# Second attention: two of the three row products of the RMS norm on GpSimd become one scaled copy with bias on ScalarE

## The chip, the cores and the metric

The kernel runs on one core of a Trainium2 chip. The metric is the device time of one execution in microseconds (us), lower is better. Engines are named as the profile has them: PE is TensorE (PEld its weight loads), DVE is VectorE, ACT is ScalarE, POOL is GpSimd, SP is SyncE, whose queue (SPq) issues every DMA of this kernel.

## What is computed

The reference is a stream of 32 batches of 112 rows by 256 features through four layers:

```
x = x + attention_1(layernorm(x), ctx)          # one head of 256
x = x + ffn_1(layernorm(x))                     # three blocks of two quantised layers with adapters
x = x + attention_2(ctx, layernorm(x))          # x gives the queries, ctx (375 rows) keys and values, 16 heads of 16
x = x + ffn_2(layernorm(x))                     # ternary weights, 256 -> 1024 -> 256
```

What the change touches is the entry of ffn_2. Its input is normalised twice, by the layer norm of the stream and by the RMS norm inside the first bitlinear:

```
x_hat = (x - mean) / sqrt(var + 1e-5)                    # layernorm
v     = mean(x_hat ** 2)
y     = x_hat * rsqrt(v + 1e-8) * norm1_w                # rmsnorm, then rounding to 8 bit levels
```

For one row both norms together are y = (x * rs - mean * rs) * norm1_w, with one scalar rs for each row that comes from mean and var alone.

## The kernel before

The kernel is written out by hand, engine by engine: each engine has its own program, and counting semaphores tie them. It has four stages with a barrier between them, except that stage 4 (ffn_2) follows on stage 3 (attention_2) without one. In the profiled execution stage 3 lies from about 700 to 1100 us, and stage 4 from there to the end.

Stage 3 is a loop over the 32 batches, `step3(b, ...)` on PE, ACT and DVE, `moves(b)` on SP and `rows3(b)` on GpSimd, with three buffers of keys and queries (`ks`, `qs`). In one step of batch b:

- PE makes the scores of batch b for 12 units u = 0 to 11 (4 heads by 125 context rows each; line 1751), and, between them, the scores of batches b + 1 and b + 2 from which the row maxima are taken (`scores_for_max`, line 1735); it weighs the values with the exponentials, two units at a time (`weigh`, line 1765; the last pair of a step is units 10 and 11), and finishes batch b - 1 (transposes, and the product with w_out, lines 1776, 1782, 1495).
- ACT makes the exponentials, one instruction for each unit (`exps`, line 954). Between them it copies the weighed values of b - 1 out (`pv_out`, line 958, ahead of u = 0), the turned heads (`o_out`, line 962, after u = 3) and the rows of negated maxima of b + 1 (`m_out`, line 966, after u = 8).
- DVE takes the 16 row maxima (line 1281), normalises the heads of b - 1, adds them to the stream (`x4`, line 1306), and takes the statistics of the new rows (`stats4`, `aggregate4`, `keep4`, lines 1311, 1316, 1320).
- SP, in this order: `rows_m(b + 1)` (waits for `m_out`), 12 loads of the keys and queries of b + 3 (`load_half`, lines 510 and 513), `store_y(b - 2)` (line 538), `store_x(b - 1)` (line 532).
- GpSimd: `norm_y` of a batch, `lay_v` (the values of a batch to come are laid out, line 728, and the output bias is added to its rows, line 732), `factors4` (eight small products that make rs and mean * rs of a batch, lines 746 to 753, each waiting for the one in front).

The row b of the stream `xs` is stored to DRAM as x (for the last residual), then normalised in place, and stored again as y (`normed_rows_dram`). `norm_y(b)` makes the three products in place, and its first one waits until the store of x has landed (semaphore `x_stored`). Stage 4 reads y and x back as tiles of 128 rows. The last steps of stage 3 hand over to stage 4: `store_y(28)` comes in SP's order ahead of the loads of the ffn_2 weights (`ternary_w_dram`), for which PE's first transpose of stage 4 (`in_turn(0)`, line 1828) waits. ACT's program at the hand-over is `pv_out(31)`, `xq_out(0)`, `o_out(31)`, `relu(0)`, `xq_out(1)`, `square(0)`, and then the tiles of stage 4 (`xq_out` line 980, `relu` 993, `square` 999, `squares` 1006, `hq_out` 1011). DVE's `activate` (line 1375) waits for `square`.

The helper `apart(eng, passed)` is a semaphore increment that no one waits for; it only sets two waits apart in the instruction stream. `over_thirds` runs step 0, a loop of nine turns of three steps, and the rest (steps 28 to 31) written out.

Of the kernel before, what the change touches and what calls it, by code (L numbers as in the profile page):

```python
# [8 lines left out]
ALU = mybir.AluOpType  # L9
ACT = mybir.ActivationFunctionType  # L10
AX_X = mybir.AxisListType.X
P = 128
# [5 lines left out]
def xattn_ffn_kernel(  # L18
# [5 lines left out]
    B, L, D = x.shape  # L24
# [33 lines left out]
    with ExitStack() as ctx:  # L58
        def alloc(stack, name, shape, dt=F32):
            return stack.enter_context(nc.sbuf_tensor(name, shape, dt))  # L60

        def sb(name, shape, dt=F32):
            return alloc(ctx, name, shape, dt)

        def sem(name):
            return ctx.enter_context(nc.semaphore(name))


        xs = sb("x_stream", [L, B, D])
# [12 lines left out]
        k4 = sb("ffn2_constants", [P, 2])  # L82
        eps4 = sb("eps4", [P, 2])
        ones3 = sb("ones3", [P, L], BF16)

# [101 lines left out]
        at = [0]  # L187
# [85 lines left out]
        def sems(names):  # L273
            return [sem(n) for n in names.split()]
# [12 lines left out]
        passed_pool, passed_dve, passed_sp = sems("passed_pool passed_dve passed_sp")  # L287
        ENG = ("pe", "act", "dve", "pool", "sp")
        stage_done = {e: sem(f"stage_done_{e}") for e in ENG}

        def stage_end(eng, me, n):
# [49 lines left out]
            "x_plus_bout_made pads_zeroed ffn2_row_factor_steps")  # L341

        (x_stored, y_stored, y_tiles_in, x_tiles_in, ternary_w_stored, ffn2_weights_in, ffn2_constants_made,
         y_made, x_factor_steps, x_rounded, x_int_turned, x_intT_ready, hidden_made, relu_made,
         squares_made, activation_made, hidden_weighted, square_sum_made, hidden_root_steps,
         hidden_factor_steps, hidden_factor_made, hidden_rounded, hidden_int_turned, hidden_intT_ready,
         ffn2_out_made, result_made) = sems(
            "x_stored y_stored y_tiles_in x_tiles_in ternary_w_stored ffn2_weights_in ffn2_constants_made "
            "y_made x_factor_steps x_rounded x_int_turned x_intT_ready hidden_made relu_made "
            "squares_made activation_made hidden_weighted square_sum_made hidden_root_steps "  # L350
            "hidden_factor_steps hidden_factor_made hidden_rounded hidden_int_turned hidden_intT_ready "
            "ffn2_out_made result_made")
# [265 lines left out]
        def _(pool):  # L618
# [114 lines left out]
            def factors4(b):  # L733


                chained = [0]

                def link(ins):
                    chained[0] += 1
                    ins.then_inc(ffn2_row_factor_steps, 1)  # L740
                    pool.wait_ge(ffn2_row_factor_steps, 10 * b + chained[0])
                    apart(pool, passed_pool)
                v, at = mv4[:, row(b), 1], row(b)
                pool.wait_ge(ffn2_row_stats, 3 * b + 3)
                apart(pool, passed_pool)
                link(pool.tensor_tensor(t4[:, at], v, eps4[0:L, 0:1], ALU.add))
                link(pool.tensor_tensor(rs4[:, at], t4[:, at], mhalf[0:L, 0:1], ALU.pow))
                link(pool.tensor_tensor(t4[:, at], v, rs4[:, at], ALU.mult))
                link(pool.tensor_tensor(t4[:, at], t4[:, at], rs4[:, at], ALU.mult))
                link(pool.tensor_tensor(t4[:, at], t4[:, at], eps4[0:L, 1:2], ALU.add))  # L750
                link(pool.tensor_tensor(rr4[:, at], t4[:, at], mhalf[0:L, 0:1], ALU.pow))
                link(pool.tensor_tensor(rs4[:, at], rs4[:, at], rr4[:, at], ALU.mult))
                link(pool.tensor_tensor(rr4[:, at], mv4[:, row(b), 0], rs4[:, at], ALU.mult))

            def norm_y(b):

                x_row = xs[:, row(b), :].rearrange("p o d -> p (o d)")
                pool.wait_ge(x_stored, 16 * (b + 1))
                apart(pool, passed_pool)
                pool.tensor_tensor(x_row, x_row, rs4[:, row(b)].broadcast_to([L, D]), ALU.mult).then_inc(ffn2_row_factor_steps, 1)  # L760
                pool.wait_ge(ffn2_row_factor_steps, 10 * b + 9)
                apart(pool, passed_pool)
                pool.tensor_tensor(x_row, x_row, rr4[:, row(b)].broadcast_to([L, D]), ALU.subtract).then_inc(ffn2_row_factor_steps, 1)
                pool.wait_ge(ffn2_row_factor_steps, 10 * b + 10)
                apart(pool, passed_pool)
                pool.tensor_tensor(x_row, x_row, n1_bc[0:L, :], ALU.mult).then_inc(y_made, 1)


            pool.tensor_tensor(k4[:, 0:1], wmean[:, 0:1], wmean[:, 0:1], ALU.mult).then_inc(ffn2_constants_made, 1)
            pool.tensor_scalar(k4[:, 1:2], wmean[:, 1:2], 1.0 / 127.0, None, ALU.mult).then_inc(ffn2_constants_made, 1)  # L770
            pool.wait_ge(ffn2_constants_made, 2)
# [64 lines left out]
        def _(act):  # L836
# [127 lines left out]
            def m_out(b):  # L964
                act.wait_ge(minus_max_turned, b + 1)
                act.activation(mrow[:, :], M3, ACT.Copy).then_inc(minus_max_rows_ready, 1)

            def step3(b, par, n):
                if not isinstance(b, int) or b >= 1:
                    pv_out(b - 1)  # L970
                for u in range(12):
                    exps(b, u)
                    if u == 3 and (not isinstance(b, int) or b >= 1):
                        o_out(b - 1)
                    if u == 8 and (not isinstance(b, int) or b < B - 1):
                        m_out(b + 1)
            def xq_out(i, par):

                act.wait_ge(x_int_turned, i + 1)
                act.activation(xqT, XT4[par], ACT.Copy, bias=-ROUND).then_inc(x_intT_ready, 1)  # L980

            m_out(0)
            over_thirds(act, step3)
            pv_out(B - 1)
            xq_out(0, 0)
            o_out(B - 1)


            def relu(i, par):
                if not isinstance(i, int) or i >= 2:  # L990
                    act.wait_ge(hidden_weighted, i - 1)
                act.wait_ge(hidden_made, i + 1)
                act.activation(th[par], H4[par], ACT.Relu, scale=am4[par][:, 8:9]).then_inc(relu_made, 1)  # L993
# [19 lines left out]
            def step4(i, par, n):  # L1013
# [18 lines left out]
        def _(dve):  # L1032
            chain = [0]

            def link(ins):
                chain[0] += 1
                ins.then_inc(dve_setup_steps, 1)
                dve.wait_ge(dve_setup_steps, chain[0])
# [283 lines left out]
            def step3(b, par, n):  # L1322

                later = not isinstance(b, int) or b >= 1
                last = (par + 2) % 3
                for k in range(H):
                    if k < H - AHEAD:
                        if not isinstance(b, int) or b < B - 1:
                            maxima(b + 1, k + AHEAD)
                    elif not isinstance(b, int) or b < B - 2:  # L1330
                        maxima(b + 2, k - (H - AHEAD))
                    if later and k == 1:
                        norm_o(b - 1)
# [103 lines left out]
                    inverse_x(i + 3, 1 - par)  # L1437

            over_thirds(dve, step3)
            dve.wait_ge(ffn2_constants_made, 3)  # L1440
            dve.wait_ge(y_tiles_in, 16)
            for i in range(2):
                max_x(i, i)
# [462 lines left out]
```

## Time and profile before

| what | value |
|---|---|
| time, median of 3 runs | 1274.8 us (1268.82 to 1278.72) |
| time of the profiled execution | 1277.96 us, of which 1276.0 us are its span |
| granted TensorE clock, mean | 0.938 |
| busy share of the span: PE, DVE, ACT, POOL | 85%, 69%, 42%, 40% |
| stage 3 in its steady part, 750 to 1068 us: PE, DVE, ACT, POOL busy | 300.1, 277.5, 194.0, 150.3 of 318 us |
| stage 4, 1130 to 1276 us: the same | 95.0, 115.5, 118.2, 91.2 of 146 us |

The shares are read against the stage in which the change lies: there PE is busy nearly all the time and DVE close behind, and the two engines between which the change moves work (ACT and POOL) are not.

### The profile page before, as it was taken

To read this page: it belongs to the slowest core of one execution; us is meant where nothing else is said; L and a number is where in the kernel's file an instruction comes from. 1 tells how busy PE (TensorE), PEld (TensorE's weight loads), DVE (VectorE), ACT (ScalarE), POOL (GpSimd) and SP (SyncE) were. 2 spreads that over 40 slices of the span, in tenths; PEclk is the share of its full clock that TensorE was granted. 3 is DMA by queue.
4 is the path that set the end of the run, shared out by engine and by line. 5 is a ranking of instruction groups with operands and counts; after the bars stand their busy time and mean duration, and the time that the engine had idled before them with its cause. 6 is when DMAs were issued, how large, how long until landed. Compare 5 with 4: busy or idle time off the path is not lost.

```text
span 1276.0 us, 30834 instructions
## 1 busy us (share of the span) xinstructions
PE 1089.4 (85%) x9234; PEld 768.8 (60%) x9234; DVE 875.6 (69%) x2318; ACT 534.5 (42%) x953; POOL 515.3 (40%) x875
## 2 busy tenths in 40 slices
PE   3689999999999698989878499999999999766665
PEld 2577777777777466566644156666666666434444
DVE  2745666666666467676666488888888888378886
ACT  1232222222222111111114255566666656578886
POOL 0324444444443212221310503554444554476665
PEclk7599999999999799999998689999999999778998
DMA  9413333333332000000003777877777776540000
GB/s 212 125 64 91 90 90 90 90 90 90 90 90 78 18 1 0 0 0 0 1 1 84 158 141 145 156 153 154 152 158 153 159 150 133 184 139 25 25 21 33
DMA packets 121313, 116.06 MB, mean 91 GB/s; under 512 B 45075, under 2 KB 114230, under 8 KB 121270
## 3 DMA queue, kind: packets, MB, share of 16 engines
q1 hardware_dynamic: 121270, 115.55, 38.7%
q8 instruction: 20, 0.33, 0.1%
q14 instruction: 23, 0.19, 0.1%
HBM read 79.15 MB, written 36.00 MB: 90 GB/s over the span
## 4 chain that ended last, share of the span: by engine, by line
PE 50%; DVE 12%; SPq 9%; issue 9%; ACT 8%; DMA 8%; POOL 2%; DVEq 1%; POOLq 0%; ACTq 0%
PE bank L1495 23%; PE bank L1653 6%; DMA qs<-q_parts_dram 5%; PE bank L1765 4%; PE bank L1589 3%; PE bank L1751 3%; SPq L510 3%; PE bank L1735 3%; ACT v_all L1006 3%; ACT v_all L999 2%; DVE nm L1281 2%; ACT v_all L993 2%; DVE hT L1200 2%; SPq L513 2%; PE bank L1578 2%
## 5 line engine op out<-in xcount | busy, mean ns | idle before, releaser
L1281 DVE TENSOR_REDUCE nm<-bank 112x1 f32<-112x375 f32 x512 | 254.0, 540 | 40.3 <-PE bank L1735 38.5
L954 ACT ACTIVATE pT<-bank 125x448 f32<-125x448 f32 x384 | 191.6, 541 | 93.2 <-PE bank L1765 82.2
L1735 PE MATMUL bank<-ks,qs 96*128 96x375 bf16 x512 | 160.8, 337 | 25.5 <-DMA qs<-q_parts_dram 23.4
L1751 PE MATMUL bank<-qs,ks 128*128 128x112 bf16 x1536 | 139.7, 214 | 0.5 <-DMA qs<-mrow 0.5
L1751 PEld LDWEIGHTS bank<-qs,ks 128*128 128x128 bf16 x1536 | 104.7, 99 | 32.8 <-issue 17.1
L1765 PE MATMUL bank<-pT,vaug 125*32 125x112 f32 x3072 | 113.3, 265 | 0.0
L905 ACT ACTIVATE yT<-bank,bcol,gcol 128x448 f32<-128x448 f32 x48 | 32.2, 721 | 160.2 <-PE bank L1635 160.2
L1653 PE MATMUL bank<-wffT,hT 128*112 128x256 f32 x384 | 98.8, 391 | 0.0
L1765 PEld LDWEIGHTS bank<-pT,vaug 125*32 125x32 f32 x3072 | 67.0, 109 | 43.5 <-issue 31.1
L1495 PE MATMUL bank<-wv1T,ctxT 128*125 128x256 f32 x384 | 88.0, 379 | 0.0
L1495 PE MATMUL bank<-ctxT,wk1T 128*128 128x375 f32 x256 | 86.0, 478 | 0.0
L818 POOL TENSOR_TENSOR v_all<-v_all 128x1024 f32<-128x1024 f32 x28 | 66.7, 2381 | 41.1 <-DVE v_all L1375 41.1
L1495 PEld LDWEIGHTS bank<-wv1T,ctxT 128*125 128x125 f32 x384 | 71.9, 187 | 17.2
L1180 DVE BATCH_NORM_STATS2 bs<-bank 112x6 f32<-112x256 f32 x96 | 36.6, 423 | 64.4 <-PE bank L1653 64.4
L704 POOL TENSOR_SCALAR ve<-mv 112x2 f32<-112x2 f32 x48 | 10.6, 222 | 169.1 <-DVE mv L1159 169.1
L886 ACT ACTIVATE pr<-bank,ebias 112x375 f32<-112x375 f32 x32 | 18.4, 574 | 140.9 <-DVE ebias L1132 140.9
L1495 PE MATMUL bank<-yT,wffT 128*128 128x448 f32 x192 | 76.2, 540 | 0.1
L1735 PEld LDWEIGHTS bank<-ks,qs 96*128 96x128 bf16 x512 | 46.6, 98 | 48.8 <-issue 32.3
L1635 PE MATMUL bank<-ident,yn 112*128 112x112 f32 x320 | 41.8, 278 | 38.2 <-DVE yn L1189 20.7
L1653 PEld LDWEIGHTS bank<-wffT,hT 128*112 128x112 f32 x384 | 63.8, 183 | 15.6 <-issue 1.6
L1635 PEld LDWEIGHTS bank<-ident,yn 112*128 112x128 f32 x320 | 34.1, 149 | 58.2 <-DVE yn L1189 35.9
L1495 PEld LDWEIGHTS bank<-ctxT,wk1T 128*128 128x128 f32 x256 | 48.4, 189 | 32.9
(204 smaller groups left out, 2297.8 us busy)
## 6 DMA issues: line engine op xcount, KB each, us to landing
k_parts_dram<-kp SPq DMA_DIRECT2D x192, 93.8 KB, 3.5
ks<-k_parts_dram SPq DMA_DIRECT2D x64, 281.2 KB, 4.3
cnat<-in_ctx_dram SPq DMA_DIRECT2D x32, 375.0 KB
ks<-k_parts_dram SPq DMA_DIRECT2D x64, 187.5 KB, 4.1
ks<-k_parts_dram SPq DMA_DIRECT2D x64, 93.8 KB, 3.5
q_parts_dram<-qp SPq DMA_DIRECT2D x48, 112.0 KB, 2.2
qs<-q_parts_dram SPq DMA_DIRECT2D x64, 84.0 KB, 4.0
x_stream<-in_x_dram SPq DMA_DIRECT2D x4, 896.0 KB, 14.5
```

The lines of the kernel that those rows point to most:

```text
L510: sp.dma_start(ks[par][at_row:at_row + n, half * H8 * T:(half + 1) * H8 * T], one.unsqueeze(1).broadcast_to([DH, reps, H8 * T])).then_inc( ...
L818: pool.tensor_tensor(gh[par], th[par], n2_bc, ALU.mult).then_inc(hidden_weighted, 1)
L954: act.activation(pT[:, u % 4, :], B3[u % 3][0:TP], ACT.Exp).then_inc(probs_made, 1)
L1006: act.activation(sq4, uh[par], ACT.Square, scale=k4[:, 0:1], bias=abi[:, :], accum_out=am4[par][:, 3:4]).then_inc(square_sum_made, 1)
L1281: dve.tensor_reduce(nm[:, h:h + 1], A3[h % 3][0:L], AX_X, ALU.max, negate=True).then_inc(head_max_taken, 1)
L1495: last = mm(o, lhs(k), rhs(k), start=(k == 0), stop=(k == KC - 1))
L1589: last = mm(AT1[:, k, :], cnat[par][:, c, k * P:(k + 1) * P], prT[:, c, :], start=(c == 0), stop=(c == TC - 1))
L1635: last = pe.transpose(YT[s][:, c, t * L:(t + 1) * L], yn[s][:, t, c * P:(c + 1) * P], ident[0:L, 0:L])
L1653: last = mm(LIN[s][:, t, :], hT[s][:, c, t * L:(t + 1) * L], wffT[:, 2 * k, c, :], start=False, stop=(c == KC - 1))
L1735: mm(A3[h % 3], qs[par][0:KS, h * L:h * L + P], ks[par][0:KS, h * T:(h + 1) * T], start=True, stop=True).then_inc(max_scores_made, 1)
L1751: last = mm(B3[c][:, j * L:(j + 1) * L], ks[par][:, h * T + c * TP:h * T + c * TP + P], qs[par][:, h * L:(h + 1) * L], start=True, stop=True)
L1765: last = mm(PV3[32 * j:32 * j + 32, g, :], vaug[par][:, c, h * VW:h * VW + 32], pT[:, u % 4, j * L:(j + 1) * L], start=(c == 0), stop=(c = ...
```

## The change

`norm_y` on GpSimd keeps only its last product, with norm1_w. The first two (x * rs, then minus mean * rs) become one instruction on ACT, `activation(Identity, scale=rs, bias=-mean * rs)`, in place on the row of the stream, in a new function `standard(b)`. Since ACT adds its bias, `factors4` gets a ninth small product (by a constant -1.0, a third column of `k4` set by a memset). `standard(b)` waits for the nine steps of `factors4(b)` and for the landed store of x, and `norm_y(b)` waits for `standard(b)`.

`standard(b - 2)` comes in ACT's step b behind the exponential of u = 10, from b = 2 on; `standard(30)` comes after `pv_out(31)`, ahead of `xq_out(0)`; `standard(31)` after `relu(0)`, ahead of `xq_out(1)`. Since steps 0 and 1 differ now, ACT's loop is written out as steps 0 to 3, eight turns of three, and steps 28 to 31. The semaphores for `apart` are one semaphore now.

```diff
                 link(pool.tensor_tensor(rs4[:, at], rs4[:, at], rr4[:, at], ALU.mult))
-                link(pool.tensor_tensor(rr4[:, at], mv4[:, row(b), 0], rs4[:, at], ALU.mult))
+                link(pool.tensor_tensor(t4[:, at], mv4[:, row(b), 0], rs4[:, at], ALU.mult))
+                link(pool.tensor_tensor(rr4[:, at], t4[:, at], k4[0:L, 2:3], ALU.mult))
 
             def norm_y(b):
 
                 x_row = xs[:, row(b), :].rearrange("p o d -> p (o d)")
-                pool.wait_ge(x_stored, 16 * (b + 1))
-                apart(pool, passed_pool)
-                pool.tensor_tensor(x_row, x_row, rs4[:, row(b)].broadcast_to([L, D]), ALU.mult).then_inc(ffn2_row_factor_steps, 1)
-                pool.wait_ge(ffn2_row_factor_steps, 10 * b + 9)
-                apart(pool, passed_pool)
-                pool.tensor_tensor(x_row, x_row, rr4[:, row(b)].broadcast_to([L, D]), ALU.subtract).then_inc(ffn2_row_factor_steps, 1)
-                pool.wait_ge(ffn2_row_factor_steps, 10 * b + 10)
+                pool.wait_ge(rows_standard, b + 1)
                 apart(pool, passed_pool)
                 pool.tensor_tensor(x_row, x_row, n1_bc[0:L, :], ALU.mult).then_inc(y_made, 1)
...
+            def standard(b):
+
+                x_row = xs[:, row(b), :].rearrange("p o d -> p (o d)")
+                act.wait_ge(ffn2_row_factor_steps, 9 * b + 9)
+                act.sem_inc(passed_act, 1)
+                act.wait_ge(x_stored, 16 * (b + 1))
+                act.sem_inc(passed_act, 1)
+                act.activation(x_row, x_row, ACT.Identity, bias=rr4[:, row(b)], scale=rs4[:, row(b)]).then_inc(rows_standard, 1)
+
             def step3(b, par, n):
                 if not isinstance(b, int) or b >= 1:
                     pv_out(b - 1)
...
                     if u == 8 and (not isinstance(b, int) or b < B - 1):
                         m_out(b + 1)
+                    if u == 10 and (not isinstance(b, int) or b >= 2):
+                        standard(b - 2)
...
             pv_out(B - 1)
+            standard(B - 2)
             xq_out(0, 0)
             o_out(B - 1)
...
             relu(0, 0)
+            standard(B - 1)
             xq_out(1, 1)
             square(0, 0)
```

## Rows read from the trace of the kernel before

**Rows 1.** The page, busy time of each engine over the span.

```profile
PE 1089.4 (85%) x9234; PEld 768.8 (60%) x9234; DVE 875.6 (69%) x2318; ACT 534.5 (42%) x953; POOL 515.3 (40%) x875
```

**Rows 2.** Windows: start:end, its length, then busy us of each engine.

```profile
750.00:1068.00 318.00, 300.12 (x4810) 203.53 (x4809) 277.51 (x728) 193.97 (x422) 150.33 (x348) 1.00 0.76 152
1130.00:1276.00 146.00, 95.00 (x574) 62.65 (x572) 115.53 (x301) 118.21 (x150) 91.20 (x77) 0.91 0.08 27
```

**Rows 3.** Timeline of one step's end: start, us, engine, line, operation.

```profile
942.83 0.98 ACT L954 ACTIVATE pT<-bank 125x448 f32<-125x448 f32 x2 [0.30 <-PE bank L1765]
943.85 0.61 POOL L760 TENSOR_TENSOR x_stream<-x_stream,rs  x1 [3.35 <-DMA x_rows_dram<-x_stream]
944.38 0.16 DVE L1320 COPY mv<-mv 112x2 f32 x1
944.40 0.59 PE L1765 MATMUL bank<-pT,vaug 125*32 125x112 f32 x16
944.65 0.61 POOL L763 TENSOR_TENSOR x_stream<-x_stream,rr  x1 [0.18 <-POOL x_stream L760]
945.05 0.54 ACT L958 ACTIVATE pvs<-bank 128x448 f32<-128x448 f32 x1 [1.25 <-PE bank L1765]
```

**Rows 4.** Timeline of ACT: where other steps of stage 3 begin.

```profile
934.14 0.54 ACT L958 ACTIVATE pvs<-bank 128x448 f32<-128x448 f32 x1 [1.24 <-PE bank L1765]
1057.96 0.55 ACT L958 ACTIVATE pvs<-bank 128x448 f32<-128x448 f32 x1 [1.25 <-PE bank L1765]
```

**Rows 5.** Groups of instructions: count, busy us, mean ns of one.

```profile
L980 ACT ACTIVATE v_all<-bank 128x256 bf16<-128x256 f32 x28 | 10.8, 384 | 25.1 <-PE bank L1828 25.0
L999 ACT ACTIVATE v_all<-v_all 128x1024 f32<-128x1024 f32 x28 | 29.6, 1059 | 2.4
L1006 ACT ACTIVATE v_all<-v_all,act_bias_col,ffn_constants 128x1024 f32<-128x1024 f32 x28 | 34.5, 1230 | 0.0
L954 ACT ACT_TABLE_LOAD x1 | 1.3, 1283 | 0.0
```

**Rows 6.** Timeline, the same two instructions in steps 3 and 27.

```profile
785.42 0.98 ACT L954 ACTIVATE pT<-bank 125x448 f32<-125x448 f32 x2 [0.30 <-PE bank L1765]
786.13 0.61 POOL L760 TENSOR_TENSOR x_stream<-x_stream,rs 112x256 f32<-112x256 f32 x1 [5.74 <-DMA x_rows_dram<-x_stream]
...
1055.74 0.98 ACT L954 ACTIVATE pT<-bank 125x448 f32<-125x448 f32 x2 [0.30 <-PE bank L1765]
1056.73 0.61 POOL L760 TENSOR_TENSOR x_stream<-x_stream,rs  x1 [3.98 <-DMA x_rows_dram<-x_stream]
```

**Rows 7.** Timeline of step 29: the last two exponentials, GpSimd's first product.

```profile
1078.67 0.98 ACT L954 ACTIVATE pT<-bank 125x448 f32<-125x448 f32 x2 [0.30 <-PE bank L1765]
1080.68 0.61 POOL L760 TENSOR_TENSOR x_stream<-x_stream,rs 112x256 f32<-112x256 f32 x1 [5.42 <-DMA x_rows_dram<-x_stream]
```

**Rows 8.** The chain that ended last, at the hand-over: start, us, what.

```profile
1090.58 3.19 DMA normed_rows_dram<-x_stream
1095.31 8.77 DMA v_all<-ternary_w_dram
```

**Rows 9.** Timeline of the hand-over: ACT, GpSimd and DVE.

```profile
1111.46 0.38 ACT L980 ACTIVATE v_all<-bank 128x256 bf16<-128x256 f32 x1 [2.33 <-PE bank L1828]
1111.96 0.19 POOL L746 TENSOR_TENSOR t<-mv,eps 112x1 f32<-112x1 f32 x1 [4.81 <-DVE mv L1320]
1116.24 0.61 POOL L760 TENSOR_TENSOR x_stream<-x_stream,rs 112x256 f32<-112x256 f32 x1 [0.27 <-POOL rr L753]
1118.41 2.99 DVE L1375 TENSOR_SCALAR v_all<-v_all,ffn_constants,act_bias_col 128x1024 f32<-128x1024 f32 x1 [0.67 <-ACT v_all L999]
1118.50 2.34 POOL L818 TENSOR_TENSOR v_all<-v_all 128x1024 f32<-128x1024 f32 x1
```

**Rows 10.** Timeline, a step whose copy on DVE is long.

```profile
1011.75 0.61 POOL L763 TENSOR_TENSOR x_stream<-x_stream,rr  x1 [0.18 <-POOL x_stream L760]
1011.81 0.57 DVE L1320 COPY mv<-mv 112x2 f32 x1
```

More of the change, by code:

```diff
@@ L81, in xattn_ffn_kernel @@
         rs4, t4, rr4 = (sb(n, [L, B]) for n in ("rs4", "t4", "rr4"))
-        k4 = sb("ffn2_constants", [P, 2])
+        k4 = sb("ffn2_constants", [P, 3])
         eps4 = sb("eps4", [P, 2])
@@ L286, in xattn_ffn_kernel @@
             "abs_w_total_made abs_w_mean_made adapter_added")
-        passed_pool, passed_dve, passed_sp = sems("passed_pool passed_dve passed_sp")
+        passed_pool = passed_dve = passed_sp = passed_act = sem("passed")
         ENG = ("pe", "act", "dve", "pool", "sp")
@@ L343, in xattn_ffn_kernel @@
         (x_stored, y_stored, y_tiles_in, x_tiles_in, ternary_w_stored, ffn2_weights_in, ffn2_constants_made,
-         y_made, x_factor_steps, x_rounded, x_int_turned, x_intT_ready, hidden_made, relu_made,
+         y_made, rows_standard, x_factor_steps, x_rounded, x_int_turned, x_intT_ready, hidden_made, relu_made,
          squares_made, activation_made, hidden_weighted, square_sum_made, hidden_root_steps,
@@ L348, in xattn_ffn_kernel @@
             "x_stored y_stored y_tiles_in x_tiles_in ternary_w_stored ffn2_weights_in ffn2_constants_made "
-            "y_made x_factor_steps x_rounded x_int_turned x_intT_ready hidden_made relu_made "
+            "y_made rows_standard x_factor_steps x_rounded x_int_turned x_intT_ready hidden_made relu_made "
             "squares_made activation_made hidden_weighted square_sum_made hidden_root_steps "
@@ L740, in link @@
                     ins.then_inc(ffn2_row_factor_steps, 1)
-                    pool.wait_ge(ffn2_row_factor_steps, 10 * b + chained[0])
+                    pool.wait_ge(ffn2_row_factor_steps, 9 * b + chained[0])
                     apart(pool, passed_pool)
@@ L752, in factors4 @@
                 link(pool.tensor_tensor(rs4[:, at], rs4[:, at], rr4[:, at], ALU.mult))
-                link(pool.tensor_tensor(rr4[:, at], mv4[:, row(b), 0], rs4[:, at], ALU.mult))
+                link(pool.tensor_tensor(t4[:, at], mv4[:, row(b), 0], rs4[:, at], ALU.mult))
+                link(pool.tensor_tensor(rr4[:, at], t4[:, at], k4[0:L, 2:3], ALU.mult))
             def norm_y(b):
                 x_row = xs[:, row(b), :].rearrange("p o d -> p (o d)")
-                pool.wait_ge(x_stored, 16 * (b + 1))
-                apart(pool, passed_pool)
-                pool.tensor_tensor(x_row, x_row, rs4[:, row(b)].broadcast_to([L, D]), ALU.mult).then_inc(ffn2_row_factor_steps, 1)
-                pool.wait_ge(ffn2_row_factor_steps, 10 * b + 9)
-                apart(pool, passed_pool)
-                pool.tensor_tensor(x_row, x_row, rr4[:, row(b)].broadcast_to([L, D]), ALU.subtract).then_inc(ffn2_row_factor_steps, 1)
-                pool.wait_ge(ffn2_row_factor_steps, 10 * b + 10)
+                pool.wait_ge(rows_standard, b + 1)
                 apart(pool, passed_pool)
                 pool.tensor_tensor(x_row, x_row, n1_bc[0:L, :], ALU.mult).then_inc(y_made, 1)
+            pool.memset(k4[:, 2:3], -1.0).then_inc(ffn2_constants_made, 1)
             pool.tensor_tensor(k4[:, 0:1], wmean[:, 0:1], wmean[:, 0:1], ALU.mult).then_inc(ffn2_constants_made, 1)
             pool.tensor_scalar(k4[:, 1:2], wmean[:, 1:2], 1.0 / 127.0, None, ALU.mult).then_inc(ffn2_constants_made, 1)
-            pool.wait_ge(ffn2_constants_made, 2)
+            pool.wait_ge(ffn2_constants_made, 3)
             pool.tensor_tensor(k4[:, 0:1], k4[:, 0:1], asc[:, :], ALU.mult).then_inc(ffn2_constants_made, 1)
@@ L982, in _ @@
             m_out(0)
-            over_thirds(act, step3)
+            for b in range(4):
+                step3(b, b % 3, 0)
+            turns = (B - 3) // 3 - 1
+            with act.Fori(0, turns) as i:
+                for m in range(3):
+                    step3(3 * i + 4 + m, (1 + m) % 3, 0)
+            for b in range(3 * turns + 4, B):
+                step3(b, b % 3, 0)
             pv_out(B - 1)
+            standard(B - 2)
             xq_out(0, 0)
@@ L1439, in _ @@
             over_thirds(dve, step3)
-            dve.wait_ge(ffn2_constants_made, 3)
+            dve.wait_ge(ffn2_constants_made, 4)
             dve.wait_ge(y_tiles_in, 16)
```

## The prediction, as it was put on record before the run

> **What bounds the kernel now.** The page's busy shares come first [rows 1]: over the whole span ACT and GpSimd stand at 42% and 40%, which says nothing yet, since they are averages over four stages. So I read the windows next, one for the steady part of stage 3 and one for stage 4 [rows 2]. In stage 3 PE is busy 300.1 of 318 us and DVE 277.5; GpSimd is busy 150.3. Work taken from GpSimd there shortens nothing by itself. In stage 4 the fullest engine is ACT, 118.2 of 146 us, so whatever moves the start of stage 4 moves the end by as much, unless ACT finds the time again, and it has only 19% idle with a dependence behind most of it.
>
> Then the timeline of a step's end, to see where the new instruction falls [rows 3]. The last two exponentials (u = 10 and 11) start at 942.83 and end at 943.81; PE starts the last weighing pair at 944.40 and ACT copies the result out at 945.05, which begins the next step. Steps last 11.26 us on average ([rows 4]: 934.14 to 1057.96 is 11 steps), and the shortest of them 10.91 (934.14 to 945.05, [rows 3, 4]). The difference of 0.35 us is mostly waiting for the loads of keys and queries that SP issues; a delay inside PE's own work can partly hide in it.
>
> **What goes.** 32 times two products on GpSimd of 0.61 us each, with 0.19 us to the next start ([rows 3]: 943.85, 944.65), 1.6 us per batch. Nothing near the end of the chain waits for them in the steady steps: y is only stored. Gain there: nothing, and at the hand-over what is worked out below.
>
> **What comes on ACT: its length.** One instruction of 112x256 with two per-partition pointers. The trace has none. Its nearest rows are 384 ns for a 256-column copy, and for 1024 columns 1059 ns without pointers against 1230 with both [rows 5]; so 384 + 171 = 555 ns. Consecutive ACT instructions overlap by about 0.1 (two of 0.54 in 0.98, [rows 3]), so it pushes the exponential of u = 11 back by 0.45 us. Bounds 0.29 (no price for the pointers) and 0.65 (no overlap and two increments to be stepped over).
>
> **What comes on ACT: its wait.** This matters as much. `standard(b - 2)` needs the landed store of x, which until now GpSimd waited for. In ACT's order it stands at 942.83 + 0.44 = 943.27, and GpSimd's first product, released by that landing, starts at 943.85 [rows 3]: ACT would wait some 0.5 us. Read the same way over steps 3 to 27, 25 readings of which the first (0.27) and the last (0.55) are shown [rows 6], it is 0.1 to 0.9 with a median of 0.5. Behind the waiting ACT stand the exponential of u = 11, then `pv_out`, which the transposes of PE and the head norm of DVE need.
>
> **What PE feels.** The exponential of u = 11 is needed by the second half of the pair that starts at 944.40 and takes 0.59, so at about 944.65; it ends at 943.81, and a release takes under 0.1 us. Slack 0.8 us [rows 3]. Delay of a step: 0.5 + 0.45 - 0.8 = 0.15 us. It feeds back: the store of x is tied to the step before (SP waits for the maxima rows, then issues its 12 loads and the stores), so a longer step lets it land earlier against ACT's program, and the steady value is half, 0.08 us. Over 26 steps 2 us. Bounds: 0 (landing inside the slack, or hidden in the 0.35 us above), and 26 x (0.9 + 0.65 - 0.8) / 2 = 10 us.
>
> **Step 29 and the weights.** In step 29 the landing is late: the exponentials start at 1078.67, GpSimd at 1080.68 [rows 7]. Wait 1.5, delay 1.5 + 0.45 - 0.8 = 1.2 us for step 30. `y_made(28)` then hangs on ACT's step 30. Before, SP stored that y at 1090.58, the moment GpSimd's third product was done, and the weights landed at 1104.08 [rows 8]. Now `standard(28)` comes at about 1090.3, ends at 1090.8, and the one product that is left ends at 1091.6: about 1.0 us later, and so are the weights and the first tile of stage 4. GpSimd's own gain of 1.6 us per batch is used up here, since it now waits for ACT's place in the order.
>
> **The last batch.** `standard(31)` stands ahead of `xq_out(1)` and `square(0)` in ACT's queue, and waits for the factors of the last batch. These began at 1111.96 and were done at 1116.2 [rows 9], 4.28 us for eight; the ninth adds 0.4 (they average 0.54, the two powers among them longer), and the start is 1.0 later: 1117.65. ACT ends at 1118.2. Before, `xq_out(1)` ran at 1111.46, so tiles 0 and 1 wait some 6.7 us. Following the queue from there: `square(0)` to 1119.4, `activate(0)` on DVE and the rounding of tile 2 to 1120.6, its transposes to 1121.3, `xq_out(2)`, `squares(0)`, `relu(1)`, `square(1)` to 1125.2 (0.29 + 1.23 + 1.1 + 1.1 and the gaps), `activate(1)` to 1126.0. Before, `activate(1)` started at 1118.41, but took 2.99 us beside GpSimd's 2.34 us product and ended at 1121.40 [rows 9]. That collision goes, because the product of tile 0 runs at 1120.4 to 1122.7 now. Net 1126.0 - 1121.4 = 4.6 us later, the 1.0 from above in it. Stage 4 carries it to the end. Bounds 2 (the order packs better) and 7 (the collision stays).
>
> **Other edits.** The memset of the constant hides in GpSimd's wait at the start of stage 3; uncovered it is 0.2 us. The ninth product in the steady steps: GpSimd is idle 3.35 us ahead of its next batch [rows 3]; uncovered 26 x 0.4 = 10 us, but nothing waits. One semaphore for all `apart` increments and the unrolled step change no wait: nothing, bounds -1 and +1.
>
> **Sum.** 2 + 4.6 = 6.6 us on the profiled execution's 1277.96, 1284.6. That run lies 3.2 above the median of 1274.8; on the median it is 1281.4.
>
> **A rule that speaks for the change.** DVE's copy `keep4` takes 0.16 us at 944.38, between two GpSimd products, and 0.57 at 1011.81, 0.06 after one had started [rows 3, 10]: it waits for the product's end. The Trainium skill, "SBUF — State Buffer", section "Who interferes with whom", says why: a copy in the two-port mode and a GpSimd instruction take one shared port pair in turn, each for its whole length. The trace agrees. By that rule fewer products mean fewer blocks. But the one product that is left moves to 0.55 + 0.15 us behind the landing, 944.45 in this step, 0.07 behind the copy: a coin's toss whether DVE meets it in each step or never.
>
> **Rivals.**
> - *Slower by over 1%: the copy and ACT's wait together.* If the left product starts just ahead of `keep4` in each step, DVE stands for up to 0.7 us, where the rows show 0.16 now. DVE is busy 87% of this stage, so some 0.4 of it reaches PE, with the undamped wait of 0.5 + 0.45 - 0.5 (the pair's start taken as the point of need) = 0.45: 0.85 less the 0.35 that the loads hide, 0.5 x 26 = 13 us, with the hand-over 18 us: 1293. It decides once a step's delay passes 0.35 us. Against it: the feedback, and that a block now and then [rows 10] leaves its step at average length.
> - *No loss at the hand-over, no block of the copy.* SP and the loads set the steps, the collision on `activate` goes, the order packs better: 1275, -1 to +3 us. For it: the waits of stage 3 lie where slack is. Against it: `standard(31)` stands in ACT's queue in plain sight.
> - *A table load for each switch.* The exponential's table was loaded once, 1.28 us, and the copies, `relu` and squares that follow load none [rows 5]. Were Identity in another set, each `standard` would cost two loads, 2.6 us, in ACT's queue with 0.8 of slack: 30 x 1.8 = 54 us, 1329. The Trainium skill, "ScalarE: Activation LUTs", section "Table sets: the hidden batching unit", says that identity is in every set; no row of this case shows it.
> - *Faster by over 1%.* 13 us would have to come from DVE's blocked copies, and the long ones are seven of 32, 0.41 us too long in [rows 10]. Only if they upset SP's order: 1261.
>
> **How the numbers follow.** Forecast (1281, own range 1277 to 1287) 0.60; no loss 0.20; slower 0.14; table loads 0.03; faster 0.03. A difference within 1% (12.7 us) is about what a measurement of this kernel can't tell from no change. The range of 1272 to 1292 leaves out the table loads, the gain and the ends of the others. Of the forecast's 0.60 a small part lies above 1287.5, so slower is 0.18, faster 0.04, same 0.78.
>
> **What would show it.** ACT: an Identity of 0.5 to 0.6 us between u = 10 and 11, with an idle of about 0.4 on the DMA of x ahead of it. Steps of 11.3 us. `xq_out(1)` at 6 to 7 us after where it was, against a first tile 1 us later. `activate(1)` at 0.81 in place of 2.99. `keep4` says which side of the toss fell. Wrong it would be made by an Identity far from 0.55, by a landing that SP's changed timing moves, or by table loads in ACT's groups.

## The result, and the profile after

The changed kernel takes 1301.42 us (median of 6 runs, 1285.1 to 1305.2) against 1275.32 us for the one before (6 runs): a ratio of 1.0174, 95% interval 1.014 to 1.0209. That is 22 us slower by the ratio, where 6.6 were forecast (the ratio leaves out the slowest execution, 1305.2 us, which lay over 1.5% above the fastest of its kernel; the medians differ by 26.1 us). The profiled execution has a span of 1297.3 us against 1276.0.

The page after, the lines that answer to [rows 1], and the chain's shares:

```profile
PE 1088.8 (84%) x9234; PEld 767.7 (59%) x9234; DVE 899.8 (69%) x2318; ACT 553.5 (43%) x985; POOL 480.5 (37%) x844
...
PE 52%; DVE 17%; issue 12%; ACT 8%; SPq 5%; DMA 2%; POOL 2%; DVEq 1%; POOLq 0%; ACTq 0%
```

GpSimd has 35 us less work and ACT 19 more, as intended. But DVE, which the change does not touch, has 24 us more with the same 2318 instructions. In the chain DVE has 17% now (12% before), and SP's issues and the DMAs, 17% together before, have 7%: the loads no longer set the steps, DVE does.

Where the time came in, by the first and last copy of the weighed values (line 958 before, 954 after; first and last start are given behind the durations):

```profile
L954 ACT ACTIVATE pvs<-bank x32: 544/544/545, 747.7 to 1114.4; 128x448 f32<-128x448 f32 x32
```

Before, these were at 752.9 and 1099.0. So the part ahead of the first of these copies is 5.2 us shorter in this execution, the 31 steps between take 366.7 us instead of 346.1 (+20.6), and the rest up to the end of the span 182.9 instead of 177.0 (+5.9). The sum is the 21.3 us between the spans.

The same window as the first of [rows 2]:

```profile
750.00:1068.00 318.00, 286.09 (x4544) 193.91 (x4548) 286.66 (x689) 198.68 (x424) 118.48 (x311) 1.00 0.72 145
```

PE's clock is full in both. PE is busy 14 us less in the same stretch, DVE 9 us more although it got through fewer instructions (689 against 728 entries). The length of a step, from the timeline of ACT as in [rows 4]:

```profile
926.42 0.54 ACT L954 ACTIVATE pvs<-bank 128x448 f32<-128x448 f32 x1 [0.72 <-PE bank L1781]
...
1058.60 0.54 ACT L954 ACTIVATE pvs<-bank 128x448 f32<-128x448 f32 x1 [0.72 <-PE bank L1781]
```

11 steps of 12.02 us, against 11.26. They are also far more alike than before: from step 5 to 28 each is 11.99 to 12.12 us long. Now the end of one step, to be laid beside [rows 3]:

```profile
948.24 0.54 ACT L950 ACTIVATE pT<-bank 125x448 f32<-125x448 f32 x1 [0.30 <-PE bank L1781]
...
948.72 0.60 ACT L971 ACTIVATE x_stream<-x_stream,rr,rs  x1
...
949.22 0.52 ACT L950 ACTIVATE pT<-bank 125x448 f32<-125x448 f32 x1
...
949.59 0.73 POOL L761 TENSOR_TENSOR x_stream<-x_stream,n_bc 112x256 f32 x1 [5.74 <-ACT x_stream L971]
...
949.80 1.30 DVE L1336 COPY mv<-mv 112x2 f32 x1
949.81 0.59 PE L1781 MATMUL bank<-pT,vaug 125*32 125x112 f32 x16
950.26 0.82 POOL L728 COPY vaug<-v_all 125x768 f32 x1
...
951.04 0.72 POOL L732 TENSOR_TENSOR x_stream<-x_stream,bout_bc 112x256 f32 x1
...
951.61 0.33 PE L1751 MATMUL bank<-ks,qs 96*128 96x375 bf16 x1 [0.74 <-DVE nm L1297]
```

The reader is to see three things. ACT does not wait: the new instruction follows the exponential at once. It takes 0.60 us and pushes the last exponential back by 0.50. And DVE's copy `keep4`, 224 numbers, takes 1.30 us: it starts 0.21 after GpSimd's product and ends at 951.1 with GpSimd's copy of the values, which follows the product without a gap. The maxima behind it come late, and PE waits 0.74 us for one of them. GpSimd's sum of the output bias (line 732) follows its copy of the values without a gap too, and DVE's copy is through all the same. The group of this copy over all steps, before and after (count, then ns min/median/max):

```profile
L1336 DVE COPY mv<-mv x32: 159/1309/1426, 757.8 to 1126.9; 112x2 f32 x27, 112x2 f32<-112x2 f32 x5
```

Its median before was 160 ns, the sum over 32 was 8.9 us, and is 37.1 now: 28 us more on DVE, more than the whole of DVE's growth of 24.

The hand-over, against [rows 9]:

```profile
1120.43 0.36 ACT L987 ACTIVATE v_all<-bank 128x256 bf16<-128x256 f32 x1
...
1131.36 0.60 ACT L971 ACTIVATE x_stream<-x_stream,rr,rs 112x256 f32<-112x256 f32 x1 [6.85 <-POOL rr L754]
1131.87 0.36 ACT L987 ACTIVATE v_all<-bank 128x256 bf16<-128x256 f32 x1
```

```profile
1138.80 0.81 DVE L1391 TENSOR_SCALAR v_all<-v_all,ffn_constants,act_bias_col 128x1024 f32<-128x1024 f32 x1 [0.66 <-ACT v_all L1014]
```

ACT stands 6.85 us for the last factors. Counted from the last copy of weighed values, `xq_out(1)` starts at 17.5 us instead of 12.5. `activate(1)` takes 0.81 us instead of 2.99, at 24.4 instead of 19.4, so it ends 2.8 us later than before. The last `activate`, that of tile 27, is 2.9 us later: it starts 166.5 us after the last copy of weighed values, against 163.6. So 2.9 of the 5.9 us come at the hand-over. The other 2.9 come behind that last `activate`, where PE's granted clock differs between the two executions (third number from the right: 0.81 before, 0.54 after):

```profile
1262.60:1276.00 13.40, 7.10 (x47) 5.11 (x45) 7.58 (x17) 4.29 (x5) 3.66 (x4) 0.81 0.12 40
1272.20 1.05 PE L1849 MATMUL bank<-v_all 128*128 128x256 bf16 x8 [1.12 <-ACT v_all L1011]
```

```profile
1280.90:1297.20 16.30, 10.04 (x47) 6.87 (x45) 7.58 (x17) 4.30 (x6) 3.68 (x4) 0.54 0.10 34
1292.61 1.89 PE L1865 MATMUL bank<-v_all 128*128 128x256 bf16 x8 [1.12 <-ACT v_all L1026]
```

The last eight products take 1.89 us instead of 1.05, as they run at the lower of PE's two clock levels, 1.2 instead of 2.4 GHz. This does not belong to the change: the kernel before with one small edit (experiment 7) shows the same last stretch of 16.3 us at a clock of 0.55. The stretch is given apart in the table behind the experiments.

### The profile page after: what moved, and what is told of

Read it like the earlier page. It is cut to its first block, busy times and chain, and to the rows that moved or that the text cites. A ratio compares the mean times of both kernels' runs of the same rounds, so it can differ in the third digit from the quotient of the medians.

```text
span 1297.3 us, 30841 instructions
## 1 busy us (share of the span) xinstructions
PE 1088.8 (84%) x9234; PEld 767.7 (59%) x9234; DVE 899.8 (69%) x2318; ACT 553.5 (43%) x985; POOL 480.5 (37%) x844
## 4 chain that ended last, share of the span: by engine, by line
PE 52%; DVE 17%; issue 12%; ACT 8%; SPq 5%; DMA 2%; POOL 2%; DVEq 1%; POOLq 0%; ACTq 0%
PE bank L1511 24%; PE bank L1669 6%; DVE nm L1297 5%; PE bank L1781 4%; PE bank L1767 4%; PE bank L1605 3%; PE bank L1751 3%; ACT v_all L1014 2%; ACT v_all L1008 2%; DVE hT L1216 2%; ACT v_all L1021 2%; PE bank L1594 2%; DVE yn L1205 1%; POOL rs L706 1%; PE bank L1844 1%
## 5 line engine op out<-in xcount | busy, mean ns | idle before, releaser
L950 ACT ACTIVATE pT<-bank 125x448 f32<-125x448 f32 x384 | 197.0, 540 | 107.8 <-PE bank L1781 73.4
L761 POOL TENSOR_TENSOR x_stream<-x_stream,n_bc 112x256 f32 (+1 forms) x32 | 23.3, 729 | 176.1 <-ACT x_stream L971 176.1
```

The costliest lines, as they stand in the source:

```text
L950: act.activation(pT[:, u % 4, :], B3[u % 3][0:TP], ACT.Exp).then_inc(probs_made, 1)
```

## The experiments

Two theories. A: DVE's copy is caught behind GpSimd's product and the copy of the values, and DVE's late maxima set the step. B: ACT's instruction ahead of the last exponential sets the step. Step lengths below are means over the 24 steps from `pv_out(3)` to `pv_out(27)` of one profiled execution, read as the time between starts of `pv_out`; "the rest" is from the last `pv_out` to the end of the span.

**1. DVE's copy written as a reduction over one element.** All else as in the changed kernel.

```diff
-                dve.tensor_copy(mv4[:, row(b), :].rearrange("p o d -> p (o d)"), mv3[:, :]).then_inc(ffn2_row_stats, 1)
+                dve.tensor_reduce(mv4[:, row(b), :].rearrange("p o d -> p (o d)"), mv3[:, :].unsqueeze(2), AX_X,
+                                  ALU.max).then_inc(ffn2_row_stats, 1)
```

> The changed kernel, with DVE's copy of two statistics per row (0.16 us alone, 1.3 us in the changed kernel) written as a reduction over one element. Theory A (the copy waits for GpSimd's product and for the copy of the values right behind it, and that sets the step): the instruction takes 0.2 us whatever GpSimd does, a step of stage 3 falls from 12.01 to 11.3 us, and the time from 1301 to about 1283 us, with the hand-over's 5 us left. Theory B (ACT's scaled copy ahead of the last exponential sets the step): the step stays at 12.0 us and the time at 1301.

Measured: 1283.18 us, 1.0056 (1.0038 to 1.0074). Step 11.28 us, rest 180.9. The group, and one step's end:

```profile
L1336 DVE TENSOR_REDUCE mv<-mv x32: 143/145/154, 762.1 to 1112.1; 112x2 f32 x27, 112x2 f32<-112x2 f32 x5
```

```profile
942.05 0.60 ACT L971 ACTIVATE x_stream<-x_stream,rr,rs  x1 [0.28 <-DMA x_rows_dram<-x_stream]
942.56 0.52 ACT L950 ACTIVATE pT<-bank 125x448 f32<-125x448 f32 x1
942.77 0.14 DVE L1336 TENSOR_REDUCE mv<-mv 112x2 f32 x1
942.92 0.73 POOL L761 TENSOR_TENSOR x_stream<-x_stream,n_bc 112x256 f32 x1 [5.01 <-ACT x_stream L971]
```

ACT's new instruction is there in each step, here with a wait of 0.28 us for the landing, and the step is as long as before. One instruction of DVE in another form takes back 18 us. B is out for the steps. With the steps short, ACT waits for the landing again, and so the product comes mostly behind DVE's instruction; in three steps it came ahead of it, and the reduction took 0.14 to 0.15 us there too.

**2. The kernel before, with the first two row products left out and nothing on ACT.**

```diff
-                pool.tensor_tensor(x_row, x_row, rs4[:, row(b)].broadcast_to([L, D]), ALU.mult).then_inc(ffn2_row_factor_steps, 1)
-                pool.wait_ge(ffn2_row_factor_steps, 10 * b + 9)
-                apart(pool, passed_pool)
-                pool.tensor_tensor(x_row, x_row, rr4[:, row(b)].broadcast_to([L, D]), ALU.subtract).then_inc(ffn2_row_factor_steps, 1)
-                pool.wait_ge(ffn2_row_factor_steps, 10 * b + 10)
-                apart(pool, passed_pool)
...
```

> The kernel before, with the first two row products of the norm left out on GpSimd and nothing put on ACT; so y is x times the norm weight, and that part of the computation is missing. Theory A: GpSimd's one product starts where the first of three did, 1.0 us behind the start of the last two exponentials, and runs on into the copy of the values without a gap, so DVE's copy is blocked for some 1.0 us in each step; steps of 11.6 to 12.0 us and 1285 to 1297 us, slower than before with less work. Theory B: as before, 1275 us or 1 to 2 less.

Measured: 1279.25 us, 1.0026 (1.0005 to 1.0046).

```profile
L1314 DVE COPY mv<-mv x32: 158/688/1278, 763.9 to 1112.2; 112x2 f32 x27, 112x2 f32<-112x2 f32 x5
```

The median of the copy is 0.69 us without anything on ACT, and the step 11.46 us: 0.2 longer with 1.6 us less work on GpSimd per batch. The sign is A's; the size is under what I expected for it (1.0 us and 11.6 to 12.0), because the product starts some 0.9 us ahead of the copy here, so that the block is partly over. The 31 steps take 351.6 us (346.1 before), and the rest 170.7 instead of 177.0; the last `activate` starts 7.1 us sooner (156.5 us after the last `pv_out`, 163.6 before): in the hand-over the two products stood on the path.

**3. The copy of the values ahead of the norm product.**

```diff
-                if not isinstance(b, int) or b >= 1:
-                    norm_y(b - 1)
                 lay_v(b + 3, par, 1)
+                if not isinstance(b, int) or b >= 1:
+                    norm_y(b - 1)
```

> The changed kernel, with GpSimd's copy of the values and its bias sum ahead of the norm product instead of behind it. Theory A: the product stands alone, followed by small products with gaps, so DVE's copy is blocked by 0.73 us at most: 0.5 to 0.7 us instead of 1.3, steps of 11.4 to 11.7 us, 1286 to 1294 us. Theory B: 12.0 us and 1301.

Measured: 1282.64 us, 1.0052 (1.0031 to 1.0073), step 11.29 us.

```profile
L1336 DVE COPY mv<-mv x32: 155/158/704, 760.9 to 1111.6; 112x2 f32 x27, 112x2 f32<-112x2 f32 x5
```

```profile
942.21 0.52 ACT L950 ACTIVATE pT<-bank 125x448 f32<-125x448 f32 x1
942.28 0.16 DVE L1336 COPY mv<-mv 112x2 f32 x1
942.56 0.73 POOL L761 TENSOR_TENSOR x_stream<-x_stream,n_bc 112x256 f32 x1 [2.62 <-ACT x_stream L971]
```

Better than I expected of A: the copy is not shortened to the product's length but mostly free, because the product now starts 0.28 us after it. With the 0.82 us copy gone from behind the product, a caught step does not hold on: the copies of steps 10 and 11 are caught (0.70 and 0.57 us), that of step 12 is free again, and ACT waits 0.60 us for the landing there. The largest value, 0.70 us, is one product. So the pair of GpSimd instructions, not the product alone, makes the loss.

**4. The scaled copy behind the last exponential.**

```diff
-                    if u == 10 and (not isinstance(b, int) or b >= 2):
+                    if u == 11 and (not isinstance(b, int) or b >= 2):
                         standard(b - 2)
```

> The changed kernel, with the scaled copy behind the exponential of u = 11 instead of ahead of it, in ACT's idle time of 1.25 us. Theory A: GpSimd's product starts 0.2 to 0.45 us later against DVE's copy, just behind it or at the same moment: either the copy is free again (0.16 us) and the step 11.3 us, time 1281, or it is still caught and the step stays at 11.9. Theory B: the last exponential is no longer delayed, so the step is 11.3 us and the time 1281 whatever the copy takes. If the copy is 1.3 us long and the step 12.0, B is out; if the copy is short and the step short, the two aren't told apart by this run.

Measured: 1281.85 us, 1.0035 (1.0015 to 1.0056), step 11.16 us, rest 182.9.

```profile
L1336 DVE COPY mv<-mv x32: 155/157/169, 762.7 to 1108.0; 112x2 f32 x27, 112x2 f32<-112x2 f32 x5
```

Both theories allowed this outcome, so it tells nothing between them. It shows that one slot in ACT's order decides, and it keeps the rest of 182.9 us.

**5. The last batch's scaled copy behind the first tile of stage 4.** The steps as in the changed kernel.

```diff
             relu(0, 0)
-            standard(B - 1)
             xq_out(1, 1)
             square(0, 0)
-            over_tiles(act, step4, 4, 4)
+            step4(0, 0, 0)
+            standard(B - 1)
+            for i in range(1, 4):
+                step4(i, i % 2, i // 2)
...
```

> The changed kernel, with the scaled copy of the last batch moved back in ACT's order: behind xq_out(1), square(0) and the first tile's instructions of stage 4, ahead of tile 1's. The steps of stage 3 keep their 12.0 us. Theory: ACT no longer stands 6.85 us for the last factors with tiles 0 and 1 behind it, so from the last copy of weighed values to the end of the span it is 178 to 179 us instead of 182.9 (177.0 before), and the time is 1297 us. Rival: the queue only moves the wait (GpSimd waits for the last scaled copy ahead of its first product of stage 4), 1300 to 1301 us.

Measured: executions of 1303.8, 1279.81, 1303.67 and 1298.17 us. The profiled one is the first of them; its 31 steps take 367.6 us, the rest 178.4. The rest is in the range of the theory, 4.5 us less than in the changed kernel, but half of that is chance: the last `activate` starts only 2.3 us sooner (164.2 us after the last `pv_out`, 166.5 in the changed kernel), and 2.1 us lie in the last stretch, where PE's clock is 0.74 here and 0.54 there. The times are too few and too far apart for a verdict on the whole; 1279.81 us would fit a kernel whose copy is not caught, but that execution was not profiled.

**6. The changed kernel again.**

> The changed kernel itself once more, to see whether its executions fall in two groups. Theory A with a lock: once DVE's copy is caught, the step is 12.01 us, the landed store of x is never waited for, and GpSimd's product stands 0.21 us ahead of the copy in each later step, so a whole execution is either near 1300 us or, where it isn't caught, near 1283. Expected: most of the executions 1297 to 1305, and a few 1280 to 1287, with few between. Rival: a scatter around 1300 without groups.

Measured: 1306.29, 1303.58, 1300.03, 1305.19, 1290.56, 1289.63 us; with the six of the result, nine executions lie at 1299 to 1306 and three at 1285 to 1291. So there are two groups, though the lower one is some 5 us above the 1283 I expected. The trace of this kernel's new execution (span 1304.2) shows steps of 11.98 us and a copy of 1307 ns in the median. In step 3 the copy is free, with the product 0.12 us behind it, and the next step takes 10.94 us; in that next step, 4, ACT does not wait any more, the product starts 0.18 us ahead of the copy, and from there to step 29 the copy is caught. That the lower group is of executions caught late or for a part is an inference: none of these was profiled.

**7. The kernel before with the reduction.** The edit of experiment 1 on the kernel before.

> The kernel before, with DVE's copy written as a reduction. Seven of its 32 copies stood 0.46 to 1.29 us. Theory A: only these steps gain, and the loads set most steps: 11.2 us instead of 11.26, 1273 to 1275 us. Rival: the reduction is itself slower or the copy's standing cost nothing, no difference.

Measured: 1274.53 us, 0.9991 (0.9968 to 1.0014), step 11.22 us. No difference that can be told. The seven caught copies of before are 3.4 us too long together, and the interval reaches from 4 us faster to 2 us slower: so the run shows that they cost little, not that the wait for the loads hides all of it.

**8 and 9. The repairs together, and without the reduction.**

> The changed kernel with all three: the scaled copy behind the last exponential, the last batch's later in ACT's order, and DVE's copy as a reduction. Steps of 11.15 us as in the run with the first alone (342.8 us from the first to the last copy of weighed values, 346.1 before) and 178 to 179 us from there to the end: 1274 to 1277 us, level with before within 0.3%.

> As the run with all three, without the reduction. The copy was 0.16 us in every step once the scaled copy stood behind the last exponential, so the reduction has nothing left to give: the same as the run with all three, 1274 to 1277 us. If it is over 3 us slower, the copy is caught again in part of the executions.

Measured: 1279.98 us, 1.0027 (1.0005 to 1.0048), and 1278.11 us, 1.0024 (1.0004 to 1.0043). Steps 11.26 and 11.29, 31 steps 345.8 and 346.4, rest 179.6 and 179.7. The same within the noise, as expected, but 3.0 and 1.1 us above the range of 1274 to 1277. The 342.8 us of experiment 4, on which that range rested, did not come again.

**10. The scaled copies of steps 30 and 31 early.** On top of 9:

```diff
-                    if u == 11 and (not isinstance(b, int) or b >= 2):
+                    if u == (5 if isinstance(b, int) and b >= B - 2 else 11) and (not isinstance(b, int) or b >= 2):
```

> The run with the scaled copy behind the last exponential and the last batch's later, changed further in steps 30 and 31 alone: there the scaled copy stands behind the exponential of u = 5, since GpSimd's factors are done 5.0 us into step 30. Theory: y of batch 28 gates the loads of the ffn_2 weights, which gate the first tile, so this chain starts 3 us sooner; from the last copy of weighed values to the end 176 to 177 us instead of 179.7, and 1273 to 1276 us, level with before or 1 to 2 us under it. Rival: the weights' transfer itself (8.8 us) is bound by the traffic beside it, or ACT stands for the factors in step 31 with PE behind it, and nothing is gained: 1278 us.

Measured: 1274.51 us, 0.9983 (0.9943 to 1.0022). In the profiled execution the first tile's transposes start 3.4 us after the last `pv_out` (6.0 in experiment 9), but the rest is 180.1 us. Two things hide the gain. The last stretch is one of 16.3 us at a clock of 0.54 (14.2 us at 0.74 in experiment 9), which has nothing to do with the edit; up to the last `activate` it is 163.8 us against 165.5. And part of what was won was lost a few instructions on:

```profile
1112.78 0.76 POOL L761 TENSOR_TENSOR x_stream<-x_stream,n_bc 112x256 f32<-112x256 f32 x1 [2.79 <-ACT x_stream L971]
1113.50 2.34 POOL L814 TENSOR_TENSOR v_all<-v_all 128x1024 f32<-128x1024 f32 x1
```

```profile
1112.88 3.11 DVE L1392 TENSOR_SCALAR v_all<-v_all 128x256 f32<-128x256 f32 x1
```

The same catch in another place: DVE's rounding of tile 3, 0.35 us alone, starts 0.1 after GpSimd's norm product and ends with the 2.34 us product behind it.

**11. The long product ahead of the norm product.** On GpSimd, on top of 10:

```diff
+            weigh_h(0, 0)
+            norm_y(B - 1)
+            root_h(0, 0)
...
```

(`norm_y(31)` leaves its place behind `factors4(31)`, and the tiles from 1 on follow.)

> The run with the early scaled copies in steps 30 and 31, with one change more: on GpSimd the first weighting product of stage 4 (2.34 us) stands ahead of the last batch's norm product instead of right behind it. In the run before, the two stood back to back, 3.1 us, just as DVE came to the rounding of tile 3, which took 3.11 us instead of 0.35. Theory (the same catch as in stage 3): that instruction takes under 1.0 us, the span from the last copy of weighed values to the end falls from 180.2 to 177 or 178, and the time is 1271 to 1273 us, 0.2 to 0.4% under before. Rival: the long product then catches another instruction of DVE or delays the maxima of tile 0, and the time stays at 1274 to 1275 us.

Measured: 1275.79 us, 0.9985 (0.9972 to 0.9997); rest 175.2 us, below the 177 to 178 expected, and 159.7 us up to the last `activate` (163.8 in experiment 10, 163.6 before). The time is 3 us above the range of 1271 to 1273.

```profile
1114.81 2.35 POOL L815 TENSOR_TENSOR v_all<-v_all 128x1024 f32<-128x1024 f32 x1 [0.24 <-POOL rr L754]
1117.35 0.94 POOL L761 TENSOR_TENSOR x_stream<-x_stream,n_bc 112x256 f32<-112x256 f32 x1 [0.19 <-ACT x_stream L980]
```

```profile
1117.63 0.81 DVE L1401 TENSOR_SCALAR v_all<-v_all 128x256 f32<-128x256 f32 x1
```

The rounding takes 0.81 us instead of 3.11. This version carries the change and is 0.15% (2 us) under the kernel before. The interval ends at 0.9997, and it is the last of several versions tried, so the gain is not certain; that the loss of 22 us is gone is.

The steps and DVE's copy over the runs, each from one profiled execution. The rest is split at the start of the last `activate`; behind it stands PE's granted clock in that last stretch:

| kernel | copy, median us | step, us | 31 steps, us | rest, us | to the last `activate`, us | last stretch, us (clock) |
|---|---|---|---|---|---|---|
| before | 0.16 | 11.26 | 346.1 | 177.0 | 163.6 | 13.4 (0.81) |
| changed | 1.31 | 12.01 | 366.7 | 182.9 | 166.5 | 16.3 (0.54) |
| 1, reduction | 0.15 | 11.28 | 347.2 | 180.9 | 166.7 | 14.2 (0.74) |
| 2, products left out | 0.69 | 11.46 | 351.6 | 170.7 | 156.5 | 14.2 (0.74) |
| 3, values first | 0.16 | 11.29 | 348.1 | 180.8 | 166.6 | 14.2 (0.74) |
| 4, behind u = 11 | 0.16 | 11.16 | 342.8 | 182.9 | 166.6 | 16.3 (0.54) |
| 5, last batch later | 1.31 | 12.02 | 367.6 | 178.4 | 164.2 | 14.2 (0.74) |
| 7, before with reduction | 0.15 | 11.22 | 344.2 | 178.3 | 161.9 | 16.3 (0.55) |
| 8, all three | 0.15 | 11.26 | 345.8 | 179.6 | 164.1 | 15.5 (0.64) |
| 9, 4 and 5 together | 0.16 | 11.29 | 346.4 | 179.7 | 165.5 | 14.2 (0.74) |
| 10, scaled copies early | 0.16 | 11.24 | 346.0 | 180.1 | 163.8 | 16.3 (0.54) |
| 11, last version | 0.16 | 11.24 | 346.8 | 175.2 | 159.7 | 15.5 (0.63) |

## Why the prediction was wrong

**The hand-over** (4.6 us forecast, 1.0 of it from step 29) was right in mechanism: ACT's stand was forecast as some 6.7 us and is 6.85, and `activate(1)` lost its collision as said (0.81). Without the 1.0 the forecast is 3.6 us from the last copy of weighed values; measured are 2.8 at the end of `activate(1)` and 2.9 at the last `activate`. That the whole rest grew by 5.9 us, near the 4.6, is chance: half of it is PE's clock in the last stretch. Experiment 5 moved this one instruction and took 2.3 of the 2.9 us back. Step 29 came as forecast where the copy is free: in experiment 1 ACT waits 1.40 us there (1.5 forecast), and the step takes 12.14 us against 10.87 (1.2 forecast for the delay).

**ACT's instruction** was right: 0.60 us against 0.555, 0.50 into the queue against 0.45. **ACT's wait** of 0.5 us per step was right only for the kernels whose steps stay short (in experiment 1 it is 0 to 0.7 us, 0.28 in the step above); in the changed kernel it is gone, since steps of 12 us let the store land in time. The loss of PE by ACT in the steady steps, 2 us in the forecast, is not seen: the 31 steps of experiment 1 are 1.1 us over those of before, 2.0 over in steps 29 to 31 and 0.9 under in the others. With the copy free, the forecast would have held: experiment 1 is 7 us over the kernel before by its ratio, and 6.6 were forecast.

**The step that failed is the meeting of GpSimd's product and DVE's copy.** The place was named and its timing worked out to 0.07 us, as a coin's toss, and then left out of the sum. Two things were wrong with it. First, its size: I took the block as the length of the product, up to 0.7 us. But `lay_v` follows it without a gap, so DVE stands until both are done, 1.31 us in the median. Experiment 3, which puts the copy of `lay_v` ahead of the product, brings the step from 12.01 to 11.29. The trace of the kernel before held one such case, in step 2, with the third product in front:

```profile
774.75 0.73 POOL L766 TENSOR_TENSOR x_stream<-x_stream,n_bc 112x256 f32<-112x256 f32 x1 [0.18 <-POOL x_stream L763]
774.98 1.29 DVE L1320 COPY mv<-mv 112x2 f32 x1
775.42 0.83 POOL L728 COPY vaug<-v_all 125x768 f32<-125x768 f32 x1
```

So the 1.3 us could have been read before the run: the change brings just the product that stands ahead of `lay_v` to the moment at which the copy comes. Second, it is no toss. The positions feed back: a caught copy lengthens the step, a longer step lets the store land before ACT asks for it, ACT's wait vanishes, and so GpSimd's product comes still earlier against the copy, 0.21 us ahead of it in nearly every later step. I had used just this feedback to halve ACT's delay, and did not follow it on to the product. Each link of this loop is read from the traces; that it holds the loop fast is an inference, which experiment 3 supports. The rival for "slower" had the right place and the right end (1293 to the measured 1301), but with 0.4 us from DVE's block and 0.45 from an undamped ACT wait, where it was DVE's block alone, 12.01 - 11.26 = 0.75 us a step: 17.4 of the 20.6 us lie in steps 5 to 28, and 2.8 in steps 29 to 31.

**The reassurance I took from rows 10** was a wrong reading: a copy of 0.57 us is 0.41 us late, about what PE waits for the loads in a step anyway (0.35 us), and so shows nothing. A copy that is 1.15 us late is beyond that cover. Experiment 7, which takes the few caught copies of before away and gains nothing that can be told, does not speak against it.

**Table loads** did not come: ACT ran the 32 scaled copies with 0.59 to 0.60 us each, none of them with a load in front.

## What to carry to other kernels

Before work is taken from GpSimd, look at the gap it leaves: the gaps between its instructions are where DVE's copies and scalar operations slip through, and two products replaced by one, back to back with a longer instruction, can block DVE more than three with gaps did. Where two engines meet within a tenth of a microsecond in each turn of a loop, follow the feedback on the loop's length to its fixed points instead of calling it a chance, and price the caught case with everything that queues behind. The cheapest test is to write the caught instruction in a form that does not meet GpSimd (here a reduction over one element, also 0.15 us): if the time comes back, the cause is found. And where stretches of two executions are compared, set the granted clock of each beside its length.

## What the runs showed of the hardware that was not expected

- A DVE copy or scalar operation in SBUF that meets two GpSimd instructions without a gap between them waits for both: 1.30 us for a 112x2 copy behind 0.73 + 0.82 us, and 3.11 us for a 128x256 scaling behind 0.76 + 2.34 us. With a gap of 0.19 us between them (the three products before) it gets in. This is no rule for every pair: between GpSimd's copy of the values and its bias sum, which starts 0.78 us after it with no gap either, DVE's copy got in each time (in all 28 caught steps of the changed kernel, and all the copies of experiment 2 that began during the first of the two). What makes the difference no run here shows. The Trainium skill, "SBUF — State Buffer", section "Who interferes with whom", has the pair held "for the whole instruction"; the traces agree for one instruction, and show that the waiting engine is in some pairs not served between two that follow at once.
- A reduction over one element does not wait for GpSimd: 3 times in experiment 1 and 11 times in experiment 7 it began during a GpSimd product with 0.18 us or more of it left, and took 144 to 155 ns, as it did alone. In the kernels before and changed the copy took 208 to 1426 ns in such places.
- One kernel's executions fell into two groups: 1299 to 1306 us nine times, 1285 to 1291 three times, while the kernel before, over all groups of runs, lies between 1268 and 1284. That the groups are those of such a loop caught early or late is an inference.
- PE's clock in the last 13 to 16 us differed from one profiled execution to the next, between 0.54 and 0.81, and moved the end of the kernel by up to 2.9 us, with the change and without it.
